# A whitening kernel for 32 images: its matrix chain in a new order, and its half-height stores in two DMA queues

## The reference, cut to what matters

```python
mean = x1.mean(-1, keepdims=True)
xc = x1 - mean
cov = xc @ xc.transpose(0, 2, 1) / M + EPS * jnp.eye(G)
# isqrt_newton_schulz(cov, 10)
Y, Z = cov / normA, I
for _ in range(10):
    T = 0.5 * (3.0 * I - Z @ Y)
    Y = Y @ T
    Z = T @ Z
decorr = Z / jnp.sqrt(normA)
y = weight1 @ decorr @ xc + bias1
```

## Time and profile before

| what | us |
|---|---|
| median of 3 runs | 466.69 (466.63 to 466.77) |
| the profiled execution's own time | 462.93 |
| its span, first to last instruction | 461.0 |
| TensorE busy in the span | 379.3 (82%) |
| VectorE busy | 329.4 (71%) |
| ScalarE busy | 332.9 (72%) |
| GpSimd busy (issuing stores) | 56.8 (12%) |
| mean DMA rate over the span | 330 GB/s |
| mean granted TensorE clock | 0.949 |

### The profile page before, as it was taken

One profiled execution on the slowest core, in us unless ns is written; L12 is line 12 of the kernel. 1 busy time (PEld: TensorE's weight loads), 2 busy tenths in 40 slices (PEclk: granted clock), 3 DMA queues, 4 the chain that ended last, 5 costly groups with the idle time before them and its releaser, 6 DMA issues.

```text
span 461.0 us, 17013 instructions
## 1 busy us (share of the span) xinstructions
PE 379.3 (82%) x7392; PEld 271.3 (59%) x7392; DVE 329.4 (71%) x1033; ACT 332.9 (72%) x450; POOL 56.8 (12%) x108
## 2 busy tenths in 40 slices
PE   0868899898989899898989897989999897977700
PEld 0856766666657667675756665666767575633100
DVE  5767887797869777988868787779888786643000
ACT  5772478797969868787878787787878796455800
POOL 0000001111111111020111111111102011112500
PEclk9976999999999989999989999899999999999965
DMA  7999939999999999999999999999999666677990
GB/s 271 416 409 410 412 141 284 338 346 351 381 358 404 357 394 344 398 390 390 385 383 362 381 394 382 367 327 388 384 391 388 218 208 208 200 213 225 312 268 18
DMA packets 28747, 152.11 MB, mean 330 GB/s; under 512 B 3968, under 2 KB 3968, under 8 KB 20736
## 3 DMA queue, kind: packets, MB, share of 16 engines
q0 software_dynamic: 9952, 75.50, 46.6%
q1 hardware_dynamic: 18432, 75.51, 43.2%
q10 hardware_dynamic: 288, 0.01, 0.0%
HBM read 75.51 MB, written 75.50 MB: 328 GB/s over the span
## 4 chain that ended last, share of the span: by engine, by line
PE 67%; DVE 11%; ACT 8%; issue 5%; DMA 2%; POOL 1%; SPq 0%; DVEq 0%; POOLq 0%; ACTq 0%
PE cov_ps L432 29%; PE y_ps L493 25%; PE chain_ps L464 6%; ACT image L220 6%; DVE transposed L315 5%; PE chain_ps L462 2%; DMA image<-x 2%; PE cov_ps L444 1%; PE chain_ps L474 1%; POOL y L188 1%; DVE yz L353 1%; DVE t_mat L354 1%; DVE col L350 1%; ACT image L230 1%; PE chain_ps L466 1%
## 5 line engine op out<-in xcount | busy, mean ns | idle before, releaser
L315 DVE STREAM_TRANSPOSE transposed<-image 128x384 f32<-128x384 f32 x384 | 215.7, 572 | 13.5 <-ACT image L220 2.8
L230 ACT ACTIVATE image<-y_ps,y_bias 128x768 f32<-128x768 f32 x192 | 164.8, 894 | 68.4 <-PE y_ps L493 67.7
L432 PE MATMUL cov_ps<-transposed 128*64 128x65 f32 x4608 | 178.7, 231 | 5.4 <-issue 5.4
L493 PE MATMUL y_ps<-image,apply_w 64*64 64x384 f32 x1536 | 171.8, 513 | 4.4 <-issue 2.3
L432 PEld LDWEIGHTS cov_ps<-transposed 128*64 128x64 f32 x4608 | 160.9, 142 | 14.5 <-issue 6.3
L220 ACT ACTIVATE image<-image,shift 128x1152 f32<-128x1152 f32 x128 | 156.1, 1248 | 1.8 <-DMA image<-x 0.8
L493 PEld LDWEIGHTS y_ps<-image,apply_w 64*64 64x64 f32 x1536 | 58.9, 135 | 15.1 <-ACT image L230 7.6
L186 POOL DMA_DIRECT2D y<-image x34 | 19.4, 572 | 381.1 <-ACT image L230 381.1
L462 PEld LDWEIGHTS chain_ps<-yz 128*64 128x64 f32 (+1 forms) x288 | 32.8, 138 | 35.4 <-DVE yz L367 27.3
L367 DVE SCALAR_TENSOR_TENSOR yz<-yz,chain_ps 64x96 f32<-64x96 f32 x144 | 33.8, 234 | 22.9 <-PE chain_ps L464 16.9
L464 PE MATMUL chain_ps<-yz,t_mat 64*64 64x96 f32 x256 | 47.0, 265 | 3.4 <-DVE t_mat L362 3.4
(11 more groups left out here) (59 smaller groups left out, 167.1 us busy)
## 6 DMA issues: line engine op xcount, KB each, us to landing
image<-x SPq DMA_DIRECT2D x128, 576.0 KB, 11.2
y<-image POOLq DMA_DIRECT2D x31, 1152.0 KB, 8.6
y<-image POOLq DMA_DIRECT2D x62, 576.0 KB, 11.0
y<-image POOLq DMA_DIRECT2D x3, 384.0 KB, 12.2
y<-image POOLq DMA_DIRECT2D x6, 192.0 KB, 11.6
b_col<-bias ACTq DMA_DIRECT2D x4, 0.1 KB, 6.3
w_nat<-weight ACTq DMA_DIRECT2D x2, 4.0 KB, 4.3
```

Of the source, the lines that this page charges most:

```text
L230: nc.scalar.activation(xs[n % SLOTS][:, :, STRIP * q:STRIP * (q + 1)], y_ps[:, f % 2, :, 0:STRIP], ACT.Identity, bias=y_bias[:, c % 2, i:i ...
L315: nc.vector.transpose(xt[q][:, TILES // 2 * part:TILES // 2 * (part + 1), 0:CH], xs[n % SLOTS][:, h, at:at + TWELFTH]).then_inc(transposed, 1)
L432: ins = nc.tensor.matmul(cov_ps[rows, n % 2, 0:GRAM], xt[q][:, t, 0:CH], xt[q][:, t, 0:GRAM], start=q == 0 and t < 2, stop=q == IMAGE_PIEC ...
L493: ins = nc.tensor.matmul(y_ps[out_rows, f % 2, h, 0:STRIP], apply_w[rows, c % 2, i].rearrange("p k g -> p (k g)"), xs[n % SLOTS][rows, h, ...
```

## The change

The chain is two steps shorter, its steps stand in other slots, the bias's offset is made at the start of the next round, and the stores go out differently.

- **Chain.** FOLD is gone. The last step before SPREAD (now LAST) multiplies Z by the weight and by Y in one product of 64 columns, VectorE then makes two matrices of it (`t_wide` and `folded`, two operations), and SPREAD is two products instead of four.
- **Slots.** TensorE has NORM in slot 2, VectorE in slot 4, and NEXT_0 is in slot 5 for both; the steps after it follow one a slot to slot 23. On ScalarE `root` stands behind the second output of sub-round 0, `half_root` in sub-round 2.
- **Offset.** The means of the pair are gathered by one more product and copied by one more VectorE operation in GATHER. The offset is made in slot 0 of the next round, by four products of one column and one VectorE operation. ScalarE's first output of a pair waits for it (`offset_dve`), TensorE's does not. `d_mask` (L382) is gone.
- **Stores.** For the first 30 images GpSimd issues the store of the upper 64 partitions and then that of 128 partitions, and SyncE that of the lower 64 partitions, ahead of the loads into the slot of the image before. The last two images are stored by SyncE alone, image 30 whole and image 31 in three parts.

```diff
+PARTS = {IMAGES - 2: 1, IMAGES - 1: 3}
-FOLD = NEXT_0 + 1 + 2 * (NEWTON - 1)
-SPREAD = FOLD + 1
-STEP_AT = {1: NORM, 3: NEXT_0} | {t + 1: t for t in range(NEXT_0 + 1, SPREAD + 1)}
+LAST = NEXT_0 + 1 + 2 * (NEWTON - 2)
+SPREAD = LAST + 1
+OFFSET_AT, NORM_AT, NORM_OUT_AT, NEXT_0_AT = 0, 2, 4, 5
+PE_AT = {NORM_AT: NORM} | {NEXT_0_AT + t - NEXT_0: t for t in range(NEXT_0, SPREAD + 1)}
+DVE_AT = {NORM_OUT_AT: NORM} | {NEXT_0_AT + t - NEXT_0: t for t in range(NEXT_0, SPREAD + 1)}
...
         @block.sync
+            for n in range(SLOTS):
+                load(n)
+            for n in range(IMAGES - PAIR):
+                store_crossed(sp, n, slice(0, IMAGE_PIECES), 0, stored_lower[n % SLOTS])
+                if 0 < n and n - 1 + SLOTS < IMAGES:
+                    load(n - 1 + SLOTS)
+            for n in range(IMAGES - PAIR, IMAGES):
+                size = IMAGE_PIECES // PARTS[n]
+                for q in range(0, IMAGE_PIECES, size):
+                    store_plain(sp, n, slice(q, q + size), stored_last)
+                    for upper in range(2):
+                        store_crossed(sp, n, slice(q, q + size), upper, stored_last)
...
         @block.gpsimd
+            for n in range(IMAGES - PAIR):
+                store_crossed(pool, n, slice(0, IMAGE_PIECES), 1, stored[n % SLOTS][1])
+                store_plain(pool, n, slice(0, IMAGE_PIECES), stored[n % SLOTS][0])
...
         @block.scalar
-                    act.wait_ge(chain_dve, OPS_TOTAL * (c + 1))
+                    act.wait_ge(offset_dve, c + 1)
...
-                    if j == 1 and exists(c - 1):
+                    if j == 2 and exists(c - 1):
                         half_root(c - 1)
...
+                    if exists(c - 2):
+                        output(c - 2, 2 * j)
                     if j == 0 and exists(c - 1):
                         root(c - 1)
-                    if exists(c - 2):
-                        output(c - 2, 2 * j)
...
         @block.vector
+                elif t == LAST:
+                    weighted, product = product, chain_ps[0:Q, C_PRODUCT + G:C_PRODUCT + 2 * G]
+                    link(nc.vector.scalar_tensor_tensor(
+                        out=t_wide[:], in0=product.unsqueeze(1).to_broadcast([Q, 2, G]), scalar=-0.5, in1=eye15_wide[:],
+                        op0=ALU.mult, op1=ALU.add))
+                    link(nc.vector.scalar_tensor_tensor(
+                        out=folded[:], in0=weighted.unsqueeze(1).to_broadcast([Q, PAIR, G]), scalar=RSQ, in1=own,
+                        op0=ALU.mult, op1=ALU.mult))
...
+            def offset(c):
+                dve.wait_ge(offset_pe, c + 1)
+                nc.vector.tensor_scalar(y_bias[:, c % 2, :], chain_ps[:, C_OFFSET:C_OFFSET + PAIR], -1.0,
+                                        b_col[:, 0:1], ALU.mult, ALU.add).then_inc(offset_dve, 1)
...
         @block.tensor
+                elif t == LAST:
+                    ins = nc.tensor.matmul(chain_ps[0:Q, C_PRODUCT:C_PRODUCT + 2 * G], z, wyz[rows, 0:2 * G],
+                                           start=True, stop=True)
                 else:
                     for half in range(2):
+                        ins = nc.tensor.matmul(chain_ps[HALF * half:HALF * (half + 1), C_SPREAD:C_SPREAD + PAIR * G],
+                                               t_wide[:].rearrange("p k g -> p (k g)"),
+                                               folded[:].rearrange("p i g -> p (i g)"), start=True, stop=True)
...
+            def offset(c):
+                pe.wait_ge(chain_dve, OPS_TOTAL * (c + 1))
+                for half in range(2):
+                    for i in range(PAIR):
+                        ins = nc.tensor.matmul(chain_ps[HALF * half:HALF * (half + 1), C_OFFSET + i:C_OFFSET + i + 1],
+                                               apply_w[:, c % 2, i].rearrange("p k g -> p (k g)"),
+                                               means[:, c % 2, i:i + 1], start=True, stop=True)
+                ins.then_inc(offset_pe, 1)
```

More of the change, by code:

```diff
@@ L113, in whiten @@
         d_col = sb("d_col", [Q, 1])
-        d_mask = sb("d_mask", [Q, PAIR])
+        means = sb("means", [P, 2, PAIR])
         outer = sb("outer", [Q, G])
@@ L161, in quarter_of, with store_plain, store_crossed, load @@
             return xs[n % SLOTS][:, h, QUARTER * o:QUARTER * (o + 1)]
+        def store_plain(engine, n, pieces, signal):
+            engine.wait_ge(y_read, IMAGE_PIECES * n + pieces.stop)
+            cols = slice(STRIP * pieces.start, STRIP * pieces.stop)
+            engine.dma_start(out_v[n, :, 0, cols], xs[n % SLOTS][:, 0, cols]).then_inc(signal, 16)
+        def store_crossed(engine, n, pieces, upper, signal):
+            engine.wait_ge(y_read, IMAGE_PIECES * n + pieces.stop)
+            cols = slice(STRIP * pieces.start, STRIP * pieces.stop)
+            rows, channels = slice(HALF * upper, HALF * (1 + upper)), slice(HALF * (1 - upper), HALF * (2 - upper))
+            engine.dma_start(out_v[n, channels, 1, cols], xs[n % SLOTS][rows, 1, cols]).then_inc(signal, 16)
         @block.sync
         def _(sp):
-            for n in range(IMAGES):
+            def load(n):
                 for p in range(QUARTERS):
@@ L179, in _ @@
                                     pattern=[[-1, P]], channel_multiplier=1).then_inc(eye_ready, 1)
[L181 to L196, removed]
+            for n in range(IMAGES - PAIR):
+                store_crossed(pool, n, slice(0, IMAGE_PIECES), 1, stored[n % SLOTS][1])
+                store_plain(pool, n, slice(0, IMAGE_PIECES), stored[n % SLOTS][0])
+            for n in range(IMAGES - PAIR - SLOTS, IMAGES - PAIR):
                 for h in range(HALVES):
-                    stores = (IMAGES - n + SLOTS - 1) // SLOTS + (IMAGE_PIECES // 2 - 1 if n == (IMAGES - 1) % SLOTS else 0)
-                    pool.wait_ge(stored[n][h], 16 * (1 + h) * stores)
+                    pool.wait_ge(stored[n % SLOTS][h], 16 * (n // SLOTS + 1))
         @block.scalar
@@ L291, in _ @@
             dve.wait_ge(shift_mat_ready, 1)
-            for zeros in (yz, t_mat, parity):
+            for zeros in (wyz, t_mat, parity, means):
                 then(nc.vector.memset(zeros[:], 0.0))
@@ L360, in chain @@
                                                         op0=ALU.mult, op1=ALU.add))
-                elif t < FOLD and (t - NEXT_0) % 2 == 1:
+                elif t < LAST and (t - NEXT_0) % 2 == 1:
                     link(nc.vector.scalar_tensor_tensor(
@@ L398, in _ @@
                     j = s // SLOTS_A_ROUND
-                    if s in STEP_AT and exists(c - 1):
-                        chain(c - 1, STEP_AT[s])
+                    if s == OFFSET_AT and exists(c - 2):
+                        offset(c - 2)
+                    if s in DVE_AT and exists(c - 1):
+                        chain(c - 1, DVE_AT[s])
                     if s == 9 and exists(c):
@@ L506, in _ @@
                         covariance(PAIR * c + 2 * j // IMAGE_PIECES, 2 * j % IMAGE_PIECES)
-                    if s in STEP_AT and exists(c - 1):
-                        chain(c - 1, STEP_AT[s], slice(0, P) if exists(c) else slice(0, Q))
+                    if s == OFFSET_AT and exists(c - 2):
+                        offset(c - 2)
+                    if s in PE_AT and exists(c - 1):
+                        chain(c - 1, PE_AT[s], slice(0, P) if exists(c) else slice(0, Q))
                     ahead = PAIR * c + 1 + j // 3
```

92 lines of the change are left out of this document (46 added, 46 removed).

## The result

| | before | changed |
|---|---|---|
| executions timed, us | 466.63, 466.69, 466.77, 474.52 | 441.01, 437.94, 471.57, 462.37 |
| median of all, us | 466.73 | 451.69 |
| profiled execution, its span, us | 462.93, 461.0 | 441.01, 438.8 |
| mean granted TensorE clock | 0.949 | 0.954 |

The changed kernel is faster: the ratio is 0.9417, with a 95% interval of 0.9339 to 0.9495, or 439.5 us, where 440.7 was forecast. That ratio leaves out the two executions of 471.57 and 462.37 us as disturbed. The median of all four is 451.69, inside the range and 11 us above the forecast. So there are two questions: whether the gain is made as the sum said, and why the executions spread so far.

The account below looks back on a forecast made before the run. TensorE was taken as nearest its limit, with the rounds' first third set by ScalarE and NORM. Savings of 13.0 + 1.6 + 1.4 + 1.7 + 8.3 = 26.0 us gave a median of 440.7 us, range 434 to 447.

Parts of the forecast that it names:

- Slots, 13.0 us: In 14 full rounds, moving NORM and NEXT_0 starts sub-round 2 0.93 us earlier each, 13.0 us in all.
- The first rival: In the rounds, the later root takes back all that was won, rounds stay at 24.28 us; 455.3 us, chance 0.13.
- The DRAIN, 8.3 us: At the kernel's end, GpSimd's DRAIN ends under SyncE's last stores, saving 8.3 us, bounds 0 and 8.4.
- The rival in which GpSimd's DRAIN waits for SyncE's transfers: At the kernel's end, the DRAIN stays last because it waits for all transfers; 449.0 us, chance 0.08.
- The stores, 1.7 us: From image 29 on, half-height stores in two queues overlap, 6.0 us an image instead of 7.7; 1.7 us once.
- so in two queues I let them run at once, 2.36 MB at 396 GB/s: In the stores, an image's halves use other partitions and overlap, so its stores take 6.0 us.
- The clock, 1.6 us: After the start, one of three clock dips goes as half the stall goes; 1.6 us, of 0 to 5.
- the last chain, 1.4 us: In the last chain, two steps fewer and smaller gains and losses make a net 1.4 us.
- the DMA share of 1.00 ... is thus not a bound as long as a round of 9.44 MB costs less than 26.2 us: In the steady rounds, the loads' cover of 31.8 us absorbs later loads at 360 GB/s and more.
- The slower rival: In SyncE's queue, stores and loads alternate, a round costs 30.8 us, the kernel 491 us; chance 0.05.

Follow-up runs that it names:

- run 1: The changed kernel with the loads and stores queued as in the kernel before; median 456.47 us, ratio 0.9622.
- run 6: The changed kernel with the short chain in the old slots, NORM in 1 and NEXT_0 in 3, root ahead of the output; median 471.59 us, ratio 1.0125.
- run 5: The changed kernel with ScalarE's root back ahead of the second output of sub-round 0; median 458.68 us, rounds of 22.41 us.
- run 3: The kernel before with only images 30 and 31 stored by SyncE, halves in one queue; median 457.32 us, ratio 0.9724.
- run 7: The changed kernel with image 31's nine stores issued by GpSimd; median 466.38 us.
- Run 4: The changed kernel with both half-height stores of images 0 to 29 in GpSimd's queue; median 449.56 us, lowest 438.83.
- run 10: The changed kernel itself, unaltered, as a control on another chip; median 451.27 us, lowest 446.68, ratio 0.9695.
- run 9: The changed kernel without the half-height stores of images 0 to 29, a quarter of the traffic; median 422.98 us.
- runs 2: The kernel before with the changed kernel's SyncE and GpSimd loads and stores, its chain untouched; median 466.98 us, lowest 456.40.
- root-first: The changed kernel with ScalarE's root ahead of the second output of sub-round 0; medians 458.68 and 454.33 us on two chips, lowest 430.47.
- run 11: The changed kernel with ScalarE's root ahead of the output, measured again on another chip; median 454.33 us, lowest 430.47.

## Why the prediction was right, and where not

**Slots, 13.0 us: right.** Measured 14 x (24.28 - 23.20) = 15.1 us if all rounds were undisturbed. Up to the last chain's gather the profiled execution is 404.67 - 388.93 = 15.7 us ahead (the gather's first product on TensorE), where 13.0 and the clock's 1.6 were forecast. The mechanism stands on four readings: L507 comes 6.1 us into the round after 0.88 us of idle; the gain is there with the old queues (run 1); it goes when the steps go back to their slots (run 6); and the rest of the stall goes when the root no longer stands behind an output (run 5). The first rival, a root too late to win anything, is out; but its cause is real and takes 0.8 us a round.

**The DRAIN, 8.3 us: right,** 8.6 with what lies around it, and shown by runs 1, 3 and 7. Its own length was taken as 8.4 us still and is 4.97; that costs nothing where it is hidden. The rival in which GpSimd's DRAIN waits for SyncE's transfers is out: it began at 423.9, with them under way.

**The stores, 1.7 us: right in size, wrong in cause.** The step that failed is "so in two queues I let them run at once, 2.36 MB at 396 GB/s". Image 28's three stores ran nearly alone from 403.4 to 415.4: 12.0 us for 2.36 MB. Before, in one queue, image 28 took 9.8 us (415.5 to 425.3). The two halves were issued 0.3 us apart, but they did not run at once. This is what the DMA queues moved (q1 is SyncE's, q0 GpSimd's) from 405 to 407 and from 408 to 410, where no other queue moved anything:

```profile
q1 hardware_dynamic: 48, 0.44, 114.2%
...
q0 software_dynamic: 58, 0.47, 104.6%
```

SyncE's half had the engines from 404.5 to 407.5, at 221 GB/s, and GpSimd's first packet followed at 407.5. So each half kept the engines busy by itself, at little over half of the full store's 396 GB/s. Run 4 puts the halves back into one queue and loses nothing. The rule of the Trainium skill (DMA: Bandwidth & Descriptors, Rules for kernel authors), that transfers to disjoint partition halves serialize, holds here, and I had set it below my own guess. The 1.4 us came with SyncE issuing the last two images: from image 29's last output to the last landing it is 27.3 and 27.4 us where GpSimd issues them (before, run 1), and 25.3 in run 3, with halves in one queue. Why is not shown.

**The clock, 1.6 us, and the last chain, 1.4 us: the chain's term is mis-sized, and the clock took back more than both.** The three dips in the middle are gone in this execution (in run 10, the same kernel, there is one at 234 us again). But from its gather to the first output product of the last pair, the last chain took 23.7 us, where it took 20.1 before: 3.6 us more and not 1.4 less. In this stretch the clock stood at its lower level, half, from 388.5 to 402.2. In run 1 it was full there, and the stretch took 19.5 us. So the shorter chain gave 0.6 us, less than half of its term, and the half clock cost some 4.2, an estimate from these two stretches. Why the clock fell there is not shown. TensorE had stood idle twice shortly before, with no releaser in the profile. The timeline of TensorE:

```profile
373.15 0.57 PE L475 MATMUL cov_ps<-transposed 128*64 128x65 f32 x13 [2.05 <-issue]
```
```profile
387.96 0.54 PE L544 MATMUL y_ps<-image,apply_w 64*64 64x384 f32 x2 [1.52 <-issue]
```

In run 9, however, the clock is at half from 380.8 to 387.6, in the same part of the program, with no such wait before it. The fall comes in that part in nine of the eleven traces with the shorter chain and in none of the three with the old one.

**The near hit of the number is in part luck.** The profiled execution was forecast at 436.9 and took 441.01. In its span, 15.7 us were won up to the last chain (14.6 forecast), 3.6 lost in it (1.4 to be won), and 1.4 and 8.6 won behind it (1.7 and 8.3): a better start covered part of the loss. And only two of the four executions come near the forecast's 440.7.

**The sum against the median: 11 us short.** The failed step is "the DMA share of 1.00 ... is thus not a bound as long as a round of 9.44 MB costs less than 26.2 us". As a bound on the image data it held: the loads land in 17.2 us (median) in place of 11.2, and ScalarE's centring waited 0.6 us for them in all. What it left out is that TensorE's instructions come over the same DMA engines. The page of every run has a queue for them, with 58 packets of 16 KB (packets, MB, share):

```profile
q8 instruction: 58, 0.95, 0.8%
```

In the 14 traces a product of TensorE waited 251 times with no releaser, and each of these waits ended 1.2 to 1.6 us behind the end of one of these packets, though a packet comes only every 6.4 to 7.1 us. Each also came at the same place, within two instructions, of every 256 in TensorE's record (weight loads and products). So a packet is the next 256 instructions, and TensorE waits for it. How late the packet comes goes with the traffic. Between 60 and 340 us it starts a median 2.6 us after TensorE has passed the place before in run 9, and 3.6 to 4.3 us in all versions that move all the data. The DMA share is 0.97 to 1.01 in those and issue 6 to 33 us; in run 9 they are 0.82 and 0.9 us, with rounds as long, and the executions agree. The two waits shown above fall in stretches with a share of 0.50 and 0.15, but their packets started at 370.85 and 385.76, and in the 4 us before either the share was 0.97 and 0.96, with stores. That it is the amount of traffic and not the half-height stores that run 9 leaves out has one sign: before 60 us, with loads alone at 410 GB/s, each of the 14 traces has two such waits, run 9 too.

Not shown is that shorter rounds are to blame for more of it: runs 2, 3 and 6 have rounds of 24.1 to 24.3 us and 11.8 to 18.9 us of issue, and the kernel before has one trace only, whose 6.3 us is the lowest of the full ones. Nor do these waits alone explain the spread: between runs 10 and 9 issue falls by 15.5 us and the median by 28. What the runs do show is that some of the gain is lost in most executions: at the lowest of all chips the changed kernel stands 23 us under the kernel before (437.94 and 461.09), at the medians 15 to 16.

**The slower rival,** SyncE's queue breaking the overlap, is out: 392 GB/s in the steady part, where it needed 330, and 0.6 us of centring waiting for loads.

**Open.** Whether traffic spread out more evenly, with nothing left out, or fewer instructions of TensorE, would bring the median down to 438 us, or root-first's to 430. No run tried either.

## What to carry to other kernels

Put into the wait of a step that crosses three engines work that the waiting engine has to do anyway: this reordering gave four fifths of the rounds' gain. The shorter chain gave a fifth by itself, but it also made the room: the old chain's steps reached the round's last slot, so NEXT_0 could not have moved. Look at what stands last behind the last landing, and let the queue with the short closing work be the last. When rounds shrink, set their traffic against the best rate of the trace (9.44 MB in 23.2 us is 407 GB/s, loads alone reach 418): where the two meet, the cover of the loads does not protect TensorE, whose instructions pass through the same engines, and one execution is no measure. Look then for waits with no releaser right behind a packet of the instruction queue.

## What was not expected of the hardware

TensorE's instructions came in packets of 16 KB, one for every 256 of them, through the same DMA engines as the images. With these engines full a packet came late often enough to stop TensorE for 6 to 33 us of an execution, in waits of up to 7.4 us (run 11), which the profile puts down to nothing.

GpSimd's DRAIN at the block's end goes with the number of DMAs that GpSimd has issued: 2511 ns after 30, 4966 after 60, 5701 after 69, 7416 after 90 and 8396 after 102, that is 82 ns for each. It does not wait for the transfers of others (at 423.9 it began with SyncE's under way, and was over before they landed), and costs nothing where another queue ends later.

Stores of 64 partitions ran at 221 and 235 GB/s with the 16 engines' share above 1, one after the other though issued from two queues 0.3 us apart, where mixed traffic reached 392. And SyncE's last nine issues took up to 2.65 us each while its earlier stores were under way.
